# Numbering the expert result rows partition first and storing the output by token, in a fused convolution, attention and expert block

## What is computed

```
x = x + conv(groupnorm(x))                    # depthwise 3x3, weights 1
t = tokens(x)                                 # (32, 256, 64)
t = t + attention(layernorm(t))               # 4 hashes x 8 buckets, 8 heads, and its own MLP
t = t + experts(layernorm(t))                 # top 2 of 8 experts, hidden size 682
x = from_tokens(t)                            # back to (32, 64, 16, 16)
```

## Time and profile before

| | |
|---|---|
| three runs | 907.57, 909.45 and 909.9 us; median 909.45 us |
| the profiled execution | 908.37 us, of which its span (first to last instruction) 906.6 us |
| busy share of the span | TensorE 78%, VectorE 56%, ScalarE 37%, GpSimd 40% |
| moved by DMA | 75.47 MB, mean 83 GB/s over the span |
| attention stage | 0 to about 497 us |
| expert stage | about 522 to 871 us |
| closing stage | 876.8 to 906.6 us, 29.8 us |

### The profile page before, as it was taken

The page is one execution under the profiler, slowest core; times in us unless marked ns, Lnnn a source line. Parts: engine busy times, 40 slices in busy tenths (PEclk is TensorE's granted clock), DMA queues, the critical chain, the costliest instruction groups (busy, mean ns, idle before and its releaser), DMA issues.

```text
span 906.6 us, 13941 instructions
## 1 busy us (share of the span) xinstructions
PE 704.3 (78%) x4664; PEld 530.9 (59%) x4664; DVE 504.8 (56%) x1246; ACT 331.7 (37%) x605; POOL 363.7 (40%) x353
## 2 busy tenths in 40 slices
PE   3577789696877978679540099999999999999943
PEld 3365668565665756548330067767776776776722
DVE  2467566766857666664431045566556556556534
ACT  0122424234233424322320045455555555555512
POOL 1213040544727174561846604334434433433430
PEclk9685858567585857655555589999999999999975
DMA  2000000010100000000104345546556555555429
GB/s 75 0 13 12 1 0 12 4 39 15 44 4 30 16 24 24 19 30 0 42 24 105 121 128 151 166 144 188 157 166 178 148 173 157 162 169 176 130 56 225
DMA packets 61975, 75.47 MB, mean 83 GB/s; under 512 B 23872, under 2 KB 48480, under 8 KB 61904
## 3 DMA queue, kind: packets, MB, share of 16 engines
q1 hardware_dynamic: 50000, 59.21, 22.7%
q0 software_dynamic: 8640, 12.74, 4.3%
q10 hardware_dynamic: 3264, 2.63, 1.0%
HBM read 58.54 MB, written 16.47 MB: 83 GB/s over the span
## 4 chain that ended last, share of the span: by engine, by line
PE 48%; issue 34%; DVE 7%; POOL 4%; DMA 3%; SPq 2%; ACT 1%; POOLq 0%; DVEq 0%
PE bk L716 22%; PE bk L727 11%; PE bk L704 3%; DMA res<-expert_results 2%; POOL expert_rows L474 2%; PE bk L534 2%; PE bk L734 2%; PE bk L612 1%; PE bk L594 1%; PE bk L638 1%; PE bk L558 1%; PE bk L551 1%; PE bk L532 1%; PE bk L630 1%; PE bk L581 1%
## 5 line engine op out<-in xcount | busy, mean ns | idle before, releaser
L1202 DVE TENSOR_TENSOR units<-bk,silu 128x512 f32<-128x512 f32 x213 | 147.3, 692 | 180.4 <-ACT silu L880 158.5
L500 POOL DMA_INDIRECT expert_results<-yout,xin x142 | 139.7, 984 | 218.8 <-DVE yout L1213 191.4
L716 PE MATMUL bk<-xs,wbuf 64*128 64x256 f32 x1704 | 205.0, 387 | 1.4 <-ACT xs L867 1.1
L716 PEld LDWEIGHTS bk<-xs,wbuf 64*128 64x128 f32 x1704 | 160.5, 188 | 44.7 <-issue 25.4
L880 ACT ACTIVATE silu<-bk 128x512 f32<-128x512 f32 x213 | 127.2, 597 | 87.7 <-PE bk L716 75.6
L474 POOL DMA_INDIRECT expert_rows<-srow,pos x128 | 131.6, 1028 | 39.5 <-issue 39.5
L727 PE MATMUL bk<-units,wbuf 128*64 128x256 f32 x852 | 107.6, 388 | 0.0
L441 POOL TENSOR_TENSOR rc<-vare_c,c_mhalf 128x8 f32<-128x8 f32 x16 | 27.7, 1733 | 174.6 <-DVE vare_c L1060 174.6
L612 PE MATMUL bk<-vblk,prob_t 128*128 128x72 f32 x256 | 49.3, 356 | 39.7 <-DVE att L1047 31.9
L727 PEld LDWEIGHTS bk<-units,wbuf 128*64 128x64 f32 x852 | 54.8, 136 | 32.4 <-issue 11.7
L612 PEld LDWEIGHTS bk<-vblk,prob_t 128*128 128x128 f32 x256 | 45.5, 264 | 47.1 <-issue 33.3
(11 more groups left out here) (184 smaller groups left out, 1055.8 us busy)
## 6 DMA issues: line engine op xcount, KB each, us to landing
wbuf<-in_weights SPq DMA_DIRECT2D x71, 576.0 KB
xin<-expert_rows SPq DMA_DIRECT2D x71, 130.0 KB, 2.2
res<-expert_results SPq DMA_DIRECT2D x16, 256.0 KB, 4.1
expert_results<-yout,xin POOLq DMA_INDIRECT x142
xg<-in_x SPq DMA_DIRECT2D x8, 256.0 KB
expert_rows<-srow,pos POOLq DMA_INDIRECT x128
out<-og ACTq DMA_DIRECT2D x8, 256.0 KB, 3.2
expert_rows<-const SPq DMA_DIRECT2D x5, 130.0 KB
```

Of the source, the lines that this page charges most:

```text
L500: g.indirect_dma_start(results[:, :], bass.IndirectOffsetOnAxis(ap=xin[:, t % X_SLOTS, h, ROW - 1:ROW].bitcast(U32), axis=0), yout[:, t % ...
L716: last = mm(bank[:, ch * MT:(ch + 1) * MT], wbuf[part, t % W_SLOTS, at:at + P], xs[part, t % 2, :], start=True, stop=True)
L1202: tt(units[:, t % 2, q, :], h3_ps[q], silu[:, q, :], ALU.mult).then_inc(unit_ready, 1)
```

## The change

The number of a result row is now k*T + d*1024 + p*8 + j: the eight token columns of a partition are neighbours in `expert_results`, so a load has one contiguous run of 512 floats (2048 bytes) per partition. There are four slots for these loads instead of two; they lie in the memory of `srow`, which is free by then. The loads of the second choice are issued by ScalarE's queue, which for this waits for all scatters itself. The transposes and the copies from PSUM are gone: the output tensor is `(NG, P, NJ, C)`, by token, VectorE's second addition writes a tile `t4` of four slots, and ScalarE's queue stores that as it is, in runs of 2048 bytes. The host brings the output into the form (32, 64, 16, 16).

```diff
-        res = sb("res", [P, 2, 2, NJ, C])
+        res = srow[:, :, :, :, :].rearrange("p g k j w -> p (g k j w)")[:, 0:RES_SLOTS * 2 * NJ * C]\
+            .rearrange("p (b k j c) -> p b k j c", b=RES_SLOTS, k=2, c=C)
-        og = sb("og", [P, 2, 2 * N])
+        t4 = sb("t4", [P, 4, NJ, C])
...
@@ sync
-            res_v = results.rearrange("(k i j p) c -> i k p j c", k=2, i=NG, p=P)
+            res_v = results.rearrange("(k i p j) c -> i k p (j c)", k=2, i=NG, p=P)
             for i in range(NG):
-                wait(sp, t3_sum, i - 1)
-                for k in range(2):
-                    sp.dma_start(res[:, i % 2, k, :, :], res_v[i, k]).then_inc(res_loaded[i % 2], 16)
+                wait(sp, t3_sum, i - RES_SLOTS + 1)
+                sp.dma_start(res[:, i % RES_SLOTS, 0, :, :].rearrange("p j c -> p (j c)"), res_v[i, 0])\
+                    .then_inc(res_loaded[i % RES_SLOTS], 16)
@@ gpsimd, row_destinations
-                g.iota(srow[:, d % ROW_SLOTS, :, :, ROW - 1].bitcast(U32), [[T, 2], [P, NJ]], base=d * GT,
-                       channel_multiplier=1).then_inc(dest_ready, 1)
+                g.iota(srow[:, d % ROW_SLOTS, :, :, ROW - 1].bitcast(U32), [[T, 2], [1, NJ]], base=d * GT,
+                       channel_multiplier=NJ).then_inc(dest_ready, 1)
@@ tensor
-            for i in range(NG):
-                pe.wait_ge(t3_ready, i + 1)
-                wait(pe, og_ready, i - 1)
-                for a in range(4):
-                    last = turn(bk12[:, i % 2, a * P:(a + 1) * P], t3[:, i % 2, 2 * a:2 * a + 2, :], ident)
-                last.then_inc(o_turned, 1)
@@ scalar
+            for b in range(X_SLOTS):
+                act.wait_ge(y_scattered[b], 32 * ((NT - b + X_SLOTS - 1) // X_SLOTS))
+            res_1 = results.rearrange("(k i p j) c -> i k p (j c)", k=2, i=NG, p=P)
+
+            def load_second(i):
+                wait(act, t3_sum, i - RES_SLOTS + 1)
+                act.dma_start(res[:, i % RES_SLOTS, 1, :, :].rearrange("p j c -> p (j c)"), res_1[i, 1])\
+                    .then_inc(res_loaded[i % RES_SLOTS], 16)
+
+            for i in range(RES_SLOTS):
+                load_second(i)
             for i in range(NG):
-                act.wait_ge(o_turned, i + 1)
-                wait(act, out_stored[i % 2], 16 * (i // 2))
-                f(og[:, i % 2, :], bk12[:, i % 2, :], ACT.Copy).then_inc(og_ready, 1)
-                act.wait_ge(og_ready, i + 1)
-                act.dma_start(out_groups[i], og[:, i % 2, :].rearrange("p (s n) -> p s n", s=2))\
-                    .then_inc(out_stored[i % 2], 16)
+                if i + RES_SLOTS < NG:
+                    load_second(i + RES_SLOTS)
+                act.wait_ge(t4_ready, i + 1)
+                act.dma_start(out[i].rearrange("p j c -> p (j c)"), t4[:, i % 4, :, :].rearrange("p j c -> p (j c)"))\
+                    .then_inc(out_stored[i % 4], 16)
@@ vector
             for i in range(NG):
-                dve.wait_ge(res_loaded[i % 2], 32 * (i // 2 + 1))
-                wait(dve, o_turned, i - 1)
-                tt(t3[:, i % 2, :, :], res[:, i % 2, 0, :, :], res[:, i % 2, 1, :, :], ALU.add).then_inc(t3_sum, 1)
+                dve.wait_ge(res_loaded[i % RES_SLOTS], 32 * (i // RES_SLOTS + 1))
+                tt(t3[:, i % 2, :, :], res[:, i % RES_SLOTS, 0, :, :], res[:, i % RES_SLOTS, 1, :, :], ALU.add)\
+                    .then_inc(t3_sum, 1)
                 dve.wait_ge(t3_sum, i + 1)
-                tt(t3[:, i % 2, :, :], t3[:, i % 2, :, :], t2_all[:, i, :, :], ALU.add).then_inc(t3_ready, 1)
+                wait(dve, out_stored[i % 4], 16 * (i // 4))
+                tt(t4[:, i % 4, :, :], t3[:, i % 2, :, :], t2_all[:, i, :, :], ALU.add).then_inc(t4_ready, 1)
```

More of the change, by code:

```diff
@@ L33 @@
 X_SLOTS = 8
+RES_SLOTS = 4
 EPS = 1e-5
@@ L341, in hybrid_block @@
         yout_ready = sem("yout_ready")
-        res_loaded = [sem(f"res_loaded{b}") for b in range(2)]
+        res_loaded = [sem(f"res_loaded{b}") for b in range(RES_SLOTS)]
         t3_sum = sem("t3_sum")
[L344 to L347, removed]
+        t4_ready = sem("t4_ready")
+        out_stored = [sem(f"out_stored{b}") for b in range(4)]
         x_groups = x.rearrange("b c h w -> (b c) (h w)").rearrange("(g s p) n -> g p s n", g=NG, s=2)
-        out_groups = out.rearrange("b c h w -> (b c) (h w)").rearrange("(g s p) n -> g p s n", g=NG, s=2)
         block = ctx.enter_context(nc.Block())
@@ L885, in _ @@
             store_results(NT - 1)
-            for i in range(NG):
-                act.wait_ge(o_turned, i + 1)
-                wait(act, out_stored[i % 2], 16 * (i // 2))
-                f(og[:, i % 2, :], bk12[:, i % 2, :], ACT.Copy).then_inc(og_ready, 1)
-                act.wait_ge(og_ready, i + 1)
-                act.dma_start(out_groups[i], og[:, i % 2, :].rearrange("p (s n) -> p s n", s=2))\
-                    .then_inc(out_stored[i % 2], 16)
-            for b in range(2):
-                act.wait_ge(out_stored[b], 16 * (NG // 2))
+            for b in range(X_SLOTS):
[7 more added lines that the diff above has]
+                load_second(i)
+            for i in range(NG):
+                if i + RES_SLOTS < NG:
[3 more added lines that the diff above has]
+                    .then_inc(out_stored[i % 4], 16)
+            for b in range(4):
+                act.wait_ge(out_stored[b], 16 * (NG // 4))
         @block.vector
@@ L1332 @@
             for name, a in arrays.items()]
-    out = nc.dram_tensor("out_0", (B, C, HH, WW), F32, kind="ExternalOutput").ap()
+    out = nc.dram_tensor("out_0", (NG, P, NJ, C), F32, kind="ExternalOutput").ap()
     hybrid_block(nc, *args, out)
     r = run_bass_kernel_spmd(nc, [arrays], core_ids=[0])
-    return r.results[0]["out_0"]
+    tokens = np.asarray(r.results[0]["out_0"]).reshape(NG, P, GB // 2, 2, 2, C)
+    return np.ascontiguousarray(tokens.transpose(0, 2, 4, 5, 3, 1)).reshape(B, C, HH, WW)
```

## The result

The changed kernel takes 899.35 us in the median (898.52 to 899.58, four runs), the kernel before 909.35 (907.57 to 909.9, four runs): a ratio of 0.9892, 95% interval 0.9875 to 0.9909, so 10.0 us less. The prediction was 900.5 us in a range of 897.5 to 904.5.

A forecast was written before the change was run, and what follows sets the result against it. The closing stage was taken as bound by DMA work per run of bytes. Flow start 878.0 + data 14.5 + landing 1.1 + additions 1.45 + store 2.65 = 897.7 against 906.6, 8.9 us less: 900.5 us, range 897.5 to 904.5.

The forecast's parts named there:

- Front: Start of closing stage: first load issued at 876.82 as before, data flowing 1.2 us later, at 878.0.
- Data: Closing stage's main term: all loads plus stores of groups 0 to 4, 5.5 MB at 380 GB/s, 14.5 us.
- Price per run: Closing-stage DMA: 7.2 ns a packet plus 0.038 ns a byte; 2048-byte runs give 385 GB/s, 2.04 us a group.
- Rival B: Closing-stage loads: smaller fixed packet cost, long runs give some 320 GB/s, 903.3 us; chance 0.10 (0.04 at 266 GB/s).
- D: Closing stage: slow memory, not full engines, so the change does nothing measurable, 908.5 us; chance 0.03.
- Is the flow ever dry: Closing-stage refills: group 4's load flows by 882.8, before the four queued groups run out at 883.5; covered by 0.7 us.
- VectorE's wait for a free store slot: Closing-stage additions: the store waited for is four groups, about 8 us, behind and lands in 3.2 us.
- Second queue: ScalarE's queue issuing second halves: group 0 under way after 0.38 us, removes gaps, does not shorten the end.
- Removed transposes: Transposes and PSUM copy per group: only the last time on the path, 1.8 us; otherwise hidden beside loads.
- Last store: End of the kernel: from the last store's issue to the end of the span, 2.65 us, taken over unchanged.
- Rival A: Closing-stage additions follow without a gap, VectorE the bound at 1.44 us a group, 897.5 us; chance 0.10.
- Rival C: Expert stage: scattered rows 8 KB apart land later, delaying weight loads, 912.2 us or more; chance 0.03.

The follow-up runs named there:

- b1: Changed kernel with eight slots for result loads instead of four, so no load waits for a sum; closing stage 21.1 us, median 900.15 us.
- a3: Changed kernel with both halves of the result loads on SP's queue, only stores on ScalarE's; closing stage 21.4 us, median 899.97 us.
- a4: Changed kernel with result rows numbered for load runs of 512 bytes (two tokens); closing stage 22.5 us, median 900.30 us.
- a5: Changed kernel with result rows numbered for load runs of 1024 bytes (four tokens); closing stage 20.7 us, median 898.29 us.
- e3: Kernel before with only the output by token, no transposes or PSUM copies, two store slots; closing stage 27.9 us, median 907.40 us.
- b3: Kernel before with 2048-byte runs and four load slots, keeping transposes, copies, two `og` slots and one queue; closing stage 25.2 us, median 903.34 us.

## Why the prediction was right

The mechanism was right: full engines, a price per run of bytes, and enough slots to keep them fed. The number came out as near as it did, 20.0 us of closing stage for 20.9, partly because two errors in the main term went opposite ways.

*Front* (1.2 us to the flow, 1.1 to land, first sum at 3.7): first sum at 3.55 after the issue. Right; the flow began a little later (the 88 GB/s from 878 to 879 put its beginning 1.35 us after the issue, by the prediction's own reckoning) and ran a little faster.

*Data* (5.5 MB at 380 GB/s, 14.5 us, to 892.5): the bytes were mis-sized. On ScalarE's queue only the stores of groups 0, 1 and 2 stand ahead of the last load, 0.79 MB and not 1.31, so 4.98 MB had to pass, 13.1 us at the same rate. In the trace the two queues had moved 2.10 + 2.89 = 4.99 MB by 892.3, about 13.5 us after the flow began: the dip below took back part of what the smaller load and the faster flow gave. From the first issue to the last group's first sum it was 893.45 - 877.43 = 16.0 us, against 1.2 + 14.5 + 1.1 = 16.8.

*Price per run* (385 GB/s, a pace of 2.04): 403 GB/s and 1.99 us (with the dip in it). Right in kind, and shown by four run lengths; the fixed part was 7.2 ns and measured 9.9, the part per byte 0.038 and measured 0.0348. Rival B, in which long runs give only 320 GB/s, and D are out.

*Is the flow ever dry* ("covered by 0.7 us"): this step failed. The two microseconds at 217 and 262 GB/s miss (800 - 479) / 400 = 0.8 us of flow, and b1, which refills nothing, has no such gap. It was not that the refill came late: the first sum ended at 881.67 and the four groups queued in advance, 2.10 MB, were through only at about 884.6 (1.97 MB by 884), so there were 2.9 us, and by the prediction's 1.2 us from issue to flow 1.7 would have been left over. So the 1.2 us, which was taken from idle engines, does not hold here. That the delay is longer where the engines are full is seen on another transfer: in a3 the first store was issued at 882.25 on ScalarE's queue, which held nothing else, and none of it moved before 886. With shorter runs the four groups last longer after the first sum: in a4, 3.6 us, there is no dip; in a5, 2.9 us, there is a smaller one (323 and 273 GB/s from 882 to 884). How long a refill takes to flow on full engines was not measured by itself, and why is open.

*VectorE's wait for a free store slot* ("a store lands in 3.2 us"): it was taken from the store's landing of before, but the stores now land in 5.6 us in the median, since they queue behind loads. In the changed kernel VectorE stood for the 0.69 us shown above, which cost nothing, as it then waited 0.19 us for the next load all the same. With eight load slots it became the bound.

*Second queue* (nothing but the front): measured 1.4 us in the closing stage. Too small; its cause is open.

*Removed transposes* (1.8 us, the last time only): e3 shows 1.9. Right for the kernel as it was; beside fast loads turning and the two slots of `og` would have cost 2 us more (b3).

*Last store* (2.65 us): issued after 894.86, end at 897.4, 2.5 us. Right.

*Rival A*, VectorE as the bound: true for the first four groups only (1.51 us each). *Rival C*, later landing of scattered rows: the expert stage is 337.6 to 338.0 us under either numbering.

## What to carry to other kernels

Read the share of the DMA engines beside their GB/s. A share over 1 at a low rate that holds over several microseconds (1.39 at 218 GB/s) went with short runs here, and more slots brought little until the layout in DRAM was changed; where the kernel itself writes the rows, the numbering is free. One window alone can mislead: in the dip, with long runs, it was 1.11 at 217 GB/s. A delay from issue to flow that was read on idle engines is too short for a refill on full ones. Once the runs are long, the landing time is the limit, and every buffer on the way, of loads and of stores, must be deep enough for a landing that has grown with the queue; deepening only the loads' side moves the wait to the stores. When parts of a change need each other, tests of one part alone understate them (5.1 of 9.8 us here), and taking one part out of the whole overstates them (6.4 + 7.1).

## What the runs showed of the hardware that was not expected

A packet cost 9.9 ns + 0.0348 ns a byte on each of sixteen engines for loads of 256 to 2048-byte runs, with no step at 512 bytes. Loads and stores mixed ran at 402 to 408 GB/s (changed kernel, 887 to 892), stores alone at up to 416 (b1, 892 to 893). Two queues with loads of 256 KB gave 377 to 408 GB/s from 881 to 884 where one gave 242 to 326 (a3), of which the cause is open. With the engines full, a store on a queue that held nothing else moved no byte for over 3.7 us after its issue (a3), against 1.2 us from issue to flow on idle engines.
